# Shifting the start addresses of six SBUF buffers by 16 bytes in a fused decoder layer (attention, cross product, quantised FFN)

## The reference, cut to what matters

```
q, k, v = x @ wq.T, x @ wk.T, x @ wv.T        # 32 query heads, 8 key/value heads, head size 128
s = q k' / sqrt(128), causal, window of 128 keys
x = layernorm(x + softmax(s) v @ wo.T)
x = layernorm(x + fake_quant(x) @ fake_quant(ctx_4096))
g, u = (x/128) @ w_gate.T, (x/128) @ w_up.T   # 2752 wide, ternary weights
x = layernorm(x + int8(int8(silu(g) * u) @ w_down.T))
```

## Time and profile before

| what | value |
|---|---|
| median of three executions | 1634.68 us (1634.43 to 1634.89) |
| the profiled execution | 1633.71 us, span 1631.9 us |
| busy in the span: PE, PEld, DVE, ACT, POOL | 1552.8, 1266.6, 1000.0, 664.3, 689.2 us |
| mean granted TensorE clock | 0.989 of full |

### The profile page before, as it was taken

The page is one execution under the profiler, slowest core; times in us unless marked ns, Lnnn a source line. Parts: engine busy times, 40 slices in busy tenths (PEclk is TensorE's granted clock), DMA queues, the critical chain, the costliest instruction groups (busy, mean ns, idle before and its releaser), DMA issues. The chain is left out here.

```text
span 1631.9 us, 22442 instructions
## 1 busy us (share of the span) xinstructions
PE 1552.8 (95%) x7792; PEld 1266.6 (78%) x7809; DVE 1000.0 (61%) x1575; ACT 664.3 (41%) x1329; POOL 689.2 (42%) x572
## 2 busy tenths in 40 slices
PE   7999999999999999999999999987799999999797
PEld 6888888888888888888888888864478777777543
DVE  4454454455445445435544544569878989899888
ACT  4423333152142333215214232544765564655574
POOL 3425244152342524325244252446676666666300
PEclk9999999999999999999999999998999999999999
DMA  7101100110110100011011010240113223222101
GB/s 289 47 26 65 40 27 26 51 39 13 64 39 26 64 31 34 26 51 39 13 64 39 26 65 27 73 183 1 40 39 104 97 96 103 100 95 100 52 39 66
DMA packets 28846, 98.51 MB, mean 60 GB/s; under 512 B 3584, under 2 KB 3968, under 8 KB 28800
## 3 DMA queue, kind: packets, MB, share of 16 engines
q1 hardware_dynamic: 28800, 97.93, 17.4%
HBM read 93.72 MB, written 4.19 MB: 60 GB/s over the span
## 5 line engine op out<-in xcount | busy, mean ns | idle before, releaser
L505 PE MATMUL ps<-xt_h,w_h 128*128 128x512 f32 x768 | 306.7, 399 | 8.4 <-DVE xt_l L1536 8.4
L1276 POOL TENSOR_TENSOR w_l<-w_raw,w_h 128x1024 fp32r<-128x1024 f32 x80 | 191.5, 2394 | 287.6 <-ACT w_h L846 287.6
L726 PE MATMUL ps<-xt_h,w_h 128*128 128x512 f32 x704 | 277.9, 395 | 25.5 <-ACT w_h L989 25.5
L507 PE MATMUL ps<-xt_h,w_l 128*128 128x512 f32 x768 | 300.4, 391 | 0.0
L506 PE MATMUL ps<-xt_l,w_h 128*128 128x512 f32 x768 | 300.0, 391 | 0.0
L727 PE MATMUL ps<-xt_l,w_h 128*128 128x512 f32 x704 | 275.2, 391 | 0.0
L1491 DVE TENSOR_TENSOR resid<-ps,resid 128x512 f32<-128x512 f32 x256 | 176.5, 690 | 140.3 <-PE ps L585 139.0
L1284 POOL TENSOR_TENSOR pm_l<-pt_l,upto 128x512 fp32r<-128x512 f32 x64 | 82.7, 1292 | 378.0 <-DVE pt_l L1479 375.7
L583 PE MATMUL ps<-w_h,o_h 128*128 128x512 f32 x512 | 204.4, 399 | 4.7 <-DVE resid L1491 3.3
L585 PE MATMUL ps<-w_h,o_l 128*128 128x512 f32 x512 | 201.2, 393 | 0.0
L584 PE MATMUL ps<-w_l,o_h 128*128 128x512 f32 x512 | 201.1, 393 | 0.0
(11 more groups left out here) (142 smaller groups left out, 2843.7 us busy)
## 6 DMA issues: line engine op xcount, KB each, us to landing
w_raw<-w_att SPq DMA_DIRECT2D x80, 512.0 KB, 3.3
w_raw<-w_gu SPq DMA_DIRECT2D x42, 512.0 KB, 3.3
d_raw<-w_down SPq DMA_DIRECT2D x22, 512.0 KB, 3.3
ctx_raw<-ctx_rows SPq DMA_DIRECT2D x8, 1024.0 KB, 6.3
resid<-x_cols SPq DMA_DIRECT2D x16, 256.0 KB, 6.2
resid<-x_rows SPq DMA_DIRECT2D x8, 512.0 KB, 7.4
out<-resid SPq DMA_DIRECT2D x8, 512.0 KB, 2.6
first_raw<-w_gu SPq DMA_DIRECT2D x1, 1024.0 KB, 5.0
```

What stands on the lines that cost most here:

```text
L505: pe.matmul(ps_out, wh, xt_h[:, c, rows], start=(c == 0), stop=False)
L507: last = pe.matmul(ps_out, wl, xt_h[:, c, rows], start=False, stop=(c == DC - 1))
L726: pe.matmul(dst, w, xt_h[:, c, rows], start=(c == 0), stop=False)
L1276: pool.tensor_tensor(w_l[:, w, :], w_raw[:, s % 2, :], w_h[:, w, :].bitcast(F32), ALU.subtract).then_inc(w_low, 1)
```

## The change

`place_moving` allocates a buffer that is four float32 elements (16 bytes) longer, in the same way and rounding as before, and hands out the part behind the first four. Six buffers are placed by it: `w_h`, `w_l`, `k_h`, `k_l`, `pm_h`, `pm_l`. Their data now starts at 16 modulo 64 bytes, and what is placed behind each of them moves up by 64 bytes. `xt_h`, `xt_l`, `q_h`, `q_l`, `v_h`, `v_l`, `o_h`, `o_l`, `w_raw` and all others stay at 0 modulo 64. `sample` is moved by 64 bytes to stay clear of a slot. The helper `qt` is only moved up in the file. No instruction is added, removed or moved on any engine; sizes, waits and order are the same.

```diff
+LINE = 4
...
+        def place_moving(name, shape, dtype):
+
+            size = 1
+            for n in shape[1:]:
+                size *= n
+            whole = place(name, [P, LINE + size], dtype)[:, LINE:LINE + size]
+            return whole.rearrange("p (a n) -> p a n", a=shape[1]) if len(shape) == 3 else whole
...
-        w_h = place("w_h", [P, RING, DM], F32R)
+        w_h = place_moving("w_h", [P, RING, DM], F32R)
         at_l = at[0]
-        w_l = place("w_l", [P, RING, DM], F32R)
+        w_l = place_moving("w_l", [P, RING, DM], F32R)
...
-        k_h = place("k_h", [P, TOK], F32R)
-        k_l = place("k_l", [P, TOK], F32R)
+        k_h = place_moving("k_h", [P, TOK], F32R)
+        k_l = place_moving("k_l", [P, TOK], F32R)
...
-        pm_h = place("pm_h", [P, TPB, 2, P], F32R)
-        pm_l = place("pm_l", [P, TPB, 2, P], F32R)
+        pm_h = qt(place_moving("pm_h", [P, TPB * 2 * P], F32R)).rearrange("p a (b k) -> p a b k", b=2)
+        pm_l = qt(place_moving("pm_l", [P, TPB * 2 * P], F32R)).rearrange("p a (b k) -> p a b k", b=2)
...
-        sample = place("sample", [P, 3, SAMPLE], F32, at_l + 2 * 4 * DM)
+        sample = place("sample", [P, 3, SAMPLE], F32, at_l + 2 * 4 * DM + 64)
```

More of the change, by code:

```diff
@@ L86, in place, with qt @@
             return nc.alloc_sbuf_tensor_at(name, shape, dtype, offset=offset)
+        def qt(ap):
+            return ap.rearrange("p (a k) -> p a k", a=TPB)
+        def place_moving(name, shape, dtype):
[4 more added lines that the diff above has]
+            return whole.rearrange("p (a n) -> p a n", a=shape[1]) if len(shape) == 3 else whole
         at_x = at[0]
@@ L184, in build @@
         y_ps = [bank(6), bank(7)]
-        def qt(ap):
-            return ap.rearrange("p (a k) -> p a k", a=TPB)
         consts = sem("consts")
```

## The result

The changed kernel takes 1652.96 us (1652.15 to 1653.76, four runs), against 1634.56 us before: 1.0113 times as long, interval 1.0100 to 1.0126. It is 18.4 us slower. No change had been forecast, and the time lies above the range, whose upper end was 1647 us.

The account below looks back on a forecast made before the run. PE's matmul row was taken to bound attention, a loop across engines the FFN. Terms of 0.3 us (moving operands), 0 and 0 added to the median of 1634.7 us gave 1635.0 us, no change; range 1580 to 1647 us.

Parts of the forecast that it names:

- What bounds the kernel: Attention lasts as long as PE's matmul row; FFN chunks follow a 15.86 us loop, so matmul costs count in attention only.
- Stationary operands at 16 bytes: 0: Projection and FFN weight loads stay hidden under streaming: 0 us; a projection load of 190 ns could grow 36 ns before showing.
- sign of being wrong: Any 512-column pitch leaving 225 to 229 ns, or mean lengths of lines 1276, 1387 or 846 changing over two percent.
- Moving operands at 16 bytes: 0 to 0.6 us: Output projection: 1392 matmuls cost 0 to 0.4 ns more each, 0.3 us taken; scores and values 0.
- rival 4: Slower: a partial 64-byte piece costs a whole one, 9.9 us in the output projection, 0.5 in 256-column matmuls; 1645 us, chance 0.21.
- four pairs: Stationary and moving operands the change was said to separate: w from xt, w from o, k from q, pm from v.
- Does the excess hang on the address?: FFN matmul without a load took 388 ns, bfloat16 379: some 9 of 10.8 ns excess belong to the float32 stream itself.
- Rivals 1 to 3: Three faster cases; the second: only the moving operand's start matters, output projection and narrower matmuls gain, 1607 us, chance 0.09.
- Rival 1: Phase between weight load and stream costs the excess; all pairs cured, attention 52.7 us shorter, 1582 us, chance 0.20.
- rival 3: Only matmuls that wait for their load are cured, 256 and 128 columns: 12.8 us, 1622 us, chance 0.09.
- The rule cited in the prediction: Moving operand and weights have their own SBUF read ports, and loading steals no read bandwidth from the matmul: nothing won.
- The term of ACT, POOL and VectorE: Their accesses to the six buffers: slack in attention; FFN toll up to 1.7 us, taken as 0, kept for the range.

Follow-up runs that it names:

- e6: Kernel before with w_h and w_l alone moved up 64 bytes, other attention operands in place modulo 512: 1651.23 us, 1.0099 times before.
- e7: Kernel before with w_h and w_l alone moved up 16 bytes: 1651.59 us, 1.0099 times before.
- e2: The change with a padding of 64 bytes instead of 16, so all buffers start at 0 modulo 64: 1652.55 us, 1.0103 times before.
- e9: Kernel before with k, pm and o moved up 128 bytes, w and xt staying: 1642.52 us, 1.0049 times before.
- e1: Kernel before with every SBUF buffer starting 16 bytes higher, distances between operands unchanged: 1644.04 us, 1.0053 times before.
- e8: Kernel before with k_h, k_l, pm_h and pm_l alone moved up 16 bytes: 1630.54 us, 0.9971 times before.
- e5: Kernel before with the whole layout 64 bytes higher, distances unchanged: 1634.87 us, 1.0000 times before.
- e3: The change with a padding of 32 bytes instead of 16: 1655.16 us, 1.0122 times before.

## Why the prediction was wrong

**What bounds the kernel: right.** Only attention turned 6 ns a matmul into time. In the FFN the chunk after the change lasts 15.92 us (POOL starts at 1282.24 and at 1298.16) where it lasted 15.86. The FFN as a whole grew by 2.0 us (360.3 us from first to last start of line 735, against 358.3). e6 shows best what is hidden there: 6.2 ns more on each of 704 + 704 matmuls are 8.7 us, and the FFN grew by 2.3 us. One flaw was in the reading of the earlier trace rows, "everything else is at half or less": the weight loads were busy for 903.6 of 1068 us, and it is with their addresses that the stream's pace turned out to vary.

```profile
1282.24 1.82 POOL L1396 TENSOR_SCALAR u_again<-w_h,prm 128x512 f32<-128x512 f32 x1 [4.74 <-ACT w_h L998]
1298.16 1.82 POOL L1396 TENSOR_SCALAR u_again<-w_h,prm 128x512 f32<-128x512 f32 x1 [4.76 <-ACT w_h L998]
```

**"Stationary operands at 16 bytes: 0": the step that failed.** It took a weight load for something that either fits under the stream beside it or does not, and so had a load grow by 36 ns before it showed. The loads of the projections did not grow: their median is 187 or 188 ns in both kernels. The distance between the streams did, by 5.4 ns, 2304 times: 12.4 us, two thirds of the loss. In e6 and e7, where only `w` moved, it grew by 5.7 and 4.8 ns. The prediction's own sign of being wrong, a 512-column distance outside 225 to 229 ns, is met.

**"Moving operands at 16 bytes: 0 to 0.6 us": wrong in size, and rival 4 in its reason.** The output projection lost 7.5 us. Rival 4 priced this term at 9.9 us by a cut 64-byte piece and gave 1645 us; it named the side and one of the two places. But e2, without any cut piece, costs the same as the change, and e9 slows the output projection to 232.5 ns by moving the stationary `o`, so its mechanism does not hold either; that its time lies near is luck. It also held the projections hidden, and with them the range stopped at 1647 us.

**The change moves more than it says.** The prediction read the layout modulo 64 only, and counted four pairs as separated by 16 bytes. The `_h` and the `_l` buffer of a pair are in fact 64 bytes apart in their new distances, and everything behind is moved by more: `o` by 384 bytes. e6 and e7 show that 64 bytes cost as much as 16, so these distances count too. No view of before shows them, but the diff does.

**"Does the excess hang on the address?": the evidence was weaker than it was taken for.** The last matmul before a wait took 388 ns without a load beside it, and this was read as proof that load and stream do not disturb each other. After the change the same place reads, for the last two before a wait and for the load behind:

```profile
L736 PE MATMUL ps<-xt_l,w_h x2: 396/396/397, 1314.0 to 1314.4; 128*128 128x512 f32 x2
1315.42 0.19 PEld L735 LDWEIGHTS ps<-xt_h,w_h 128*128 128x128 f32 x1 [1.04 <-issue]
```

The one that started at 1314.4 us has no load beside it either, and its record is 9 ns longer. There are 18 such places in the FFN before, all at 388 ns. After the change nine of 18 are at 388, each behind a distance of 226 or 227 ns, and nine at 392 or 397, each behind one of 232 to 234; in e6 all 17 are at 390 to 397. So the record of the last stream goes with the pace of the row before it, though no load runs beside it. Absence of a load at that moment says nothing on whether the weights' address matters. Of the excess over bfloat16 the runs say only that no layout tried brought a 512-column float32r row under a steady 226 ns; whose it is stays open.

**Rivals 1 to 3.** Rival 1 had the right kind of cause, addresses of load and stream to each other, but the layout of before was already the good one for 512 columns: of the layouts tried, only distance 0 modulo 256 with starts on multiples of 64 keeps 226.7 ns (e1 has the distance without such starts, and 230.5). Something like rival 3 happened inside the change (2.3 us won by scores and values) and is e8 alone (4.8 us), though less than its 12.8 us, and no run shows that those matmuls wait for their load. The sum had scores and values at 0. e6 differs from before in addresses alone, and its projections by 5.7 ns a matmul. The rule cited in the prediction, of the Trainium skill's "TensorE: Matmul & The Clock Gate" ("Step-by-step: what each phase is for"), has two independent read ports for the two operands; the measurement decides here: the pace of the stream does depend on where the stationary operand lies, though no run shows whether it is at the ports. e7 is a shift by exactly 16 bytes and costs 16 us. The Trainium skill's "SBUF — State Buffer" ("Specifications (TRN2)") prices crossings between 16-byte lines, and the prediction worked out from it that such a shift is free; the measurement is against that.

**The term of ACT, POOL and VectorE: right for attention, near for the FFN.** In attention the reads and writes of shifted buffers last as before: line 1285 takes 2393 ns against 2394, the copy into `w_h` has a median of 1053 ns against 1052. In the FFN the subtraction on GpSimd (line 1390 before, 1399 after), 7% of the chain that ended last, went from 1408 to 1421 ns on average, 84 times: 1.1 us. Neither of its buffers is one of the six, but `u_again` moved by 64 bytes against `w_raw`; it is at 1420 ns in e6 too, and at 1408 in e5, where both moved.

**What stays open.** What makes the distance count modulo 256, and only for float32r, why +16 helps 256 columns and hurts 512, and what takes a row into its slow pattern and out of it. The runs give the rule by the table, not the mechanism. A shift of `w` against `xt` by 128 or 256 bytes was not tried, so the period of 256 is shown by a shift for the output projection, scores and values only. (It fits the projections too: `w` lies 256 modulo 512 from `xt` and 0 from `o` in the kernel before, and both rows run at 226.7 ns.)

## What to carry to other kernels

When a row of matmuls is the bound, the layout of its operands is part of its price: keep the starts of the stationary and the moving operand equal modulo 256 bytes, and on multiples of 64, for 512-column float32r matmuls, and check that an edit in one buffer's size doesn't shift the next ones off it. For 256-column ones, try 16 bytes on the moving operand alone (0.3% here). And an odd row (one matmul without a load beside it) disproves a mechanism only if the thing it is compared with has been seen to differ.

## What the runs showed that was not expected

- A float32r row of 512-column matmuls has two steady distances, 226.7 and about 233 ns, at the same full clock, and the layout sets how often each is met: 89% fast before, 20% after, 5% in e3. The bfloat16 row with the same shift between its operands stays at 215.9 ns.
- Moving a whole layout by 64 bytes changes nothing (1.0000), by 16 bytes costs 0.5%, and moving one pair in it by 64 bytes costs 1.0%.
- Shifting the stationary operand slows a stream that has not moved, and by as much as anything else here (from 227.1 to 233.3 ns in e6's FFN).
- Shifting `k` and `pm` by 16 bytes slows the projections, which use neither, from 227.4 to 228.0 ns.
